# The first microseconds of a two-layer kernel: order of the first requests, layer 0 by chunks of the input, and finer waits

## The reference

```python
x = x + (jnp.einsum('bsd,bdh->bsh', x, W[cat_ids]) + b[cat_ids][:, None, :])      # layer 0

def _dense(x, wi_, wo_):
    return jax.nn.relu(x @ wi_) @ wo_
s0 = _dense(x, swi[0], swo[0])
s1 = _dense(x, swi[1], swo[1])
h = jax.nn.relu(jnp.einsum('bsd,bdf->bsf', x, wi[type_label]))
eo = jnp.einsum('bsf,bfd->bsd', h, wo[type_label])
gate_in = jnp.concatenate([eo[:, 0], s0[:, 0], s1[:, 0]], axis=-1)
w = jax.nn.softmax(jax.nn.relu(gate_in @ g1) @ g2, axis=-1)[:, :, None, None]
x = x + (eo * w[:, 0] + s0 * w[:, 1] + s1 * w[:, 2])                              # layer 1
```

## Time and profile before

| | |
|---|---|
| three runs, median (lowest, highest) | 270.22 us (269.86, 270.35) |
| the profiled execution | 269.85 us, of which the span is 267.9 us |
| TensorE busy | 263.4 us, 98% of the span |
| VectorE, ScalarE, GpSimd busy | 162.3, 149.8, 161.5 us |
| data moved | 18.31 MB, 68 GB/s over the span |
| granted TensorE clock | full in every slice of the span |

### The profile page before, as it was taken

How to read it: one execution, slowest core, us unless ns; L and a number is a source line. 1 busy time by engine, 2 the same in 40 slices (tenths; PEclk the granted TensorE clock), 3 DMA queues, 4 the chain that set the end, 5 groups by cost and what they waited for, 6 DMA issues and landing times.

```text
span 267.9 us, 3482 instructions
## 1 busy us (share of the span) xinstructions
PE 263.4 (98%) x1172; PEld 218.7 (82%) x1172; DVE 162.3 (61%) x246; ACT 149.8 (56%) x265; POOL 161.5 (60%) x170
## 2 busy tenths in 40 slices
PE   8999999999999999999999999999999999999995
PEld 8788888888888888888888888888888888888884
DVE  3879958634654445555345475345476577985664
ACT  2597357665665655765646645546545764645320
POOL 0179989999948949927945626626526528435000
PEclk9999999999999999999999999999999999999999
DMA  5825322022022022012022022022022022000404
GB/s 195 256 100 157 118 78 79 4 78 79 0 81 79 0 78 78 22 60 78 2 78 78 5 76 78 0 79 79 2 78 78 0 81 70 8 0 2 157 1 157
DMA packets 7473, 18.31 MB, mean 68 GB/s; under 512 B 1312, under 2 KB 2080, under 8 KB 7456
## 3 DMA queue, kind: packets, MB, share of 16 engines
q1 hardware_dynamic: 6736, 16.92, 19.2%
q10 hardware_dynamic: 720, 1.18, 1.3%
HBM read 16.00 MB, written 2.10 MB: 68 GB/s over the span
## 4 chain that ended last, share of the span: by engine, by line
PE 96%; DMA 2%; SPq 1%; DVE 0%; issue 0%; ACT 0%; DVEq 0%
PE acc L705 48%; PE chain L705 24%; PE right L705 12%; PE left L705 7%; PE acc L722 4%; DMA w_raw<-cat_w 2%; PE corner L705 1%; SPq L232 1%; DVE x L696 0%; ACT w_hi L363 0%; SPq L234 0%; DVEq L695 0%
## 5 line engine op out<-in xcount | busy, mean ns | idle before, releaser
L275 POOL TENSOR_TENSOR m_lo<-staged,m_hi 128x512 fp32r<-128x512 f32 (+1 forms) x48 | 82.2, 1721 | 78.5 <-ACT m_hi L351 63.9
L705 PE MATMUL acc<-h_hi,m_hi 128*128 128x512 f32 x190 | 73.9, 389 | 0.0
L705 PE MATMUL acc<-h_lo,m_hi 128*128 128x512 f32 x190 | 73.9, 389 | 0.0
L705 PE MATMUL acc<-h_hi,m_lo 128*128 128x512 f32 x190 | 73.9, 389 | 0.0
L375 ACT COPY kept<-chain 128x512 f32<-128x512 f32 x66 | 38.8, 588 | 55.0 <-PE chain L705 55.0
L705 PEld LDWEIGHTS acc<-h_hi,m_hi 128*128 128x128 f32 x190 | 35.7, 188 | 7.4
L705 PEld LDWEIGHTS acc<-h_lo,m_hi 128*128 128x128 f32 x190 | 35.7, 188 | 7.4
L705 PEld LDWEIGHTS acc<-h_hi,m_lo 128*128 128x128 f32 x190 | 35.7, 188 | 7.4
L492 DVE SCALAR_TENSOR_TENSOR h_lo<-left,h_hi 128x512 fp32r<-128x512 f32 x24 | 16.6, 691 | 29.1 <-ACT h_hi L387 29.1
L275 POOL TENSOR_TENSOR staged<-staged 128x128 f32<-128x128 f32 x66 | 31.0, 485 | 1.7
L497 DVE TENSOR_TENSOR left<-left,kept 128x512 f32<-128x512 f32 x22 | 15.3, 695 | 24.3 <-PE left L705 24.3
(11 more groups left out here) (111 smaller groups left out, 442.9 us busy)
## 6 DMA issues: line engine op xcount, KB each, us to landing
staged<-mlp_w SPq DMA_DIRECT2D x22, 512.0 KB, 3.3
x<-x_t ACTq DMA_DIRECT2D x4, 256.0 KB, 4.0
staged<-mlp_w SPq DMA_DIRECT2D x4, 256.0 KB, 3.6
x<-x_t SPq DMA_DIRECT2D x4, 256.0 KB, 5.2
out_t<-x SPq DMA_DIRECT2D x2, 512.0 KB, 3.3
g_sb<-g SPq DMA_DIRECT2D x1, 768.0 KB, 3.8
out_t<-x SPq DMA_DIRECT2D x3, 256.0 KB, 2.3
w_raw<-cat_w SPq DMA_DIRECT2D x4, 128.0 KB, 3.1
```

The lines of the kernel that those rows point to most:

```text
L275: return nc.gpsimd.tensor_tensor(out, a, b, ALU.subtract)
L705: last = nc.tensor.matmul(out[:, columns], half[:, slot, at:at + P], moving[:, columns], start=(start and n == 0), stop=(stop and n == 2), ...
```

## The change

Several edits, all but the last two in the first twelve microseconds:

- **Requests.** ScalarE requests x's second tile only once the first piece of x's first tile has landed, and reads the mlp id itself (a register load), so that it can request wi of group 0, between its two casts of layer 0's weights. SyncE no longer requests that wi.
- **Warm-up.** 12 matmuls instead of 16.
- **Layer 0 by chunks.** For x's first tile (`layer0_first`) both output chunks take input chunk 0 first, in the order hi x hi, hi x lo, lo x hi, each with its own wait, then input chunk 1. For the other three tiles (`layer0`) all products with x_hi come first, those with x_lo last.
- **Finer waits.** x_split becomes a semaphore per chunk. Group 0's wi is cast and split in two halves, row 1 (256 columns, `row1_hi_ready`, `row1_split`) and row 2, and the first direct products wait for part_split 1, 2 and 3 one after another.
- **Who splits.** x_lo of the second tile's second chunk goes from VectorE to GpSimd.
- **Sample 1.** VectorE's first h_lo of group 1 comes ahead of the second x1.
- **Group 3.** Four t_hi casts of the second pair, before split between the ends of groups 2 and 3, all go to group 3, the first two between the casts of hidden sums.

The gate is as it was.

```diff
-WARMUP = 16
+WARMUP = 12
...
-        x_split = [[sem(f"x_split{b}{t}") for t in range(HALVES)] for b in range(B)]
+        x_split = [[[sem(f"x_split{b}{t}{d}") for d in range(DC)] for t in range(HALVES)] for b in range(B)]
...
+        def load_wi(eng, bank, j):
+            eng.dma_start(staged[:, j % 2, A11:RAW_S], group_weights(bank, j, slice(A11, RAW_S))).then_inc(staged_loaded[j % 2], 16)
+
         def load_group(eng, bank, j):
             if j < DIRECT:
 
-                eng.dma_start(staged[:, j % 2, A11:RAW_S], group_weights(bank, j, slice(A11, RAW_S))).then_inc(staged_loaded[j % 2], 16)
+                if j:
+                    load_wi(eng, bank, j)
...
-            split_first(0, False)
+            pool.wait_ge(x_hi_ready[0], 2)
+            subtract(x_part(x_lo, 0, 1, 1), x1_part(0, 1, 1), x_part(x_hi, 0, 1, 1).bitcast(F32)).then_inc(x_split[0][1][1], 1)
+
+            pool.wait_ge(row1_hi_ready, 1)
+            subtract(m_lo[:, 0, A11:A22], staged[:, 0, A11:A22], m_hi[:, 0, A11:A22].bitcast(F32)).then_inc(row1_split, 1)
+            pool.wait_ge(m_hi_ready, first_part(0))
+            subtract(m_lo[:, 0, A22:RAW_S], staged[:, 0, A22:RAW_S], m_hi[:, 0, A22:RAW_S].bitcast(F32)).then_inc(m_split, 1)
             split_first(1, False)
...
-            load_x(act, 0, 0)
+            for d in range(DC):
+                load_x(act, 0, 0, d)
 
             act.wait_ge(ones_ready, 1)
             nc.scalar.activation(table[:], ones[:, 0:1], ACT.Relu)
-            load_x(act, 0, 1)
+            mlp = act.value_load(mlp_ids[0:1, 0:1], min_val=0, max_val=EXPERTS - 1)
+
+            act.wait_ge(x_loaded[0][0][0], 16)
             for d in range(DC):
-                w_hi_of(0, d)
+                load_x(act, 0, 1, d)
+            w_hi_of(0, 0)
+            load_wi(act, bass.ds(mlp, 1), 0)
+            w_hi_of(0, 1)
             for d in range(DC):
                 x_hi_of(0, 1, d)
-            split_first_hi(0, False)
             part_hi_of(0)
+            act.wait_ge(staged_loaded[0], 16)
+            nc.scalar.copy(m_hi[:, 0, A11:A22], staged[:, 0, A11:A22]).then_inc(row1_hi_ready, 1)
             part_hi_of(1)
+            nc.scalar.copy(m_hi[:, 0, A22:RAW_S], staged[:, 0, A22:RAW_S]).then_inc(m_hi_ready, 1)
...
+                if j == 3:
+                    t_hi_of(1, 0)
                 hidden_hi(j, 2)
+                if j == 3:
+                    t_hi_of(1, 1)
...
+                if j == 3:
+                    for n in (2, 3):
+                        t_hi_of(1, n)
-                for pair, first in ((1, 2), (2, 5), (3, 9)):
+                for pair, first in ((2, 5), (3, 9)):
...
-            for d in range(DC):
-                x_lo_of(0, 1, d)
+            x_lo_of(0, 1, 0)
...
             make_x1(1, 0, 0)
-            for i in range(4):
+            hidden_lo(1, 0)
+            make_x1(1, 0, 1)
+            for i in range(1, 4):
                 hidden_lo(1, i)
-            make_x1(1, 0, 1)
...
+            def layer0_first():
+
                 for i in range(DC):
+                    pe.wait_ge(x_first_hi, i + 1)
+                    pe.wait_ge(w_hi_ready, i + 1)
+                    for d in range(DC):
+                        layer0_product(0, 0, i, d, w_hi, x_hi, i == 0, False)
+                    pe.wait_ge(x_split[0][0][i], 1)
+                    for d in range(DC):
+                        layer0_product(0, 0, i, d, w_hi, x_lo, False, False)
+                    pe.wait_ge(w_split[0], i + 1)
+                    for d in range(DC):
+                        last = layer0_product(0, 0, i, d, w_lo, x_hi, False, i == DC - 1)
+                        if i == DC - 1:
+                            last.then_inc(layer0_done, 1)
+
+            def layer0(b, t):
+
+                for i in range(DC):
+                    if t == 0:
+                        pe.wait_ge(w_hi_ready, b * DC + i + 1)
+                        pe.wait_ge(w_split[b], i + 1)
+                    pe.wait_ge(x_hi_ready[b], b * t * DC + i + 1)
+                    for d in range(DC):
+                        layer0_product(b, t, i, d, w_hi, x_hi, i == 0, False)
+                        layer0_product(b, t, i, d, w_lo, x_hi, False, False)
+                for d in range(DC):
+                    for i in range(DC):
+                        if d == 0:
+                            pe.wait_ge(x_split[b][t][i], 1)
+                        last = layer0_product(b, t, i, d, w_hi, x_lo, False, i == DC - 1)
+                    last.then_inc(layer0_done, 1)
...
-                if i == 0:
+                if j == i == 0:
+                    pe.wait_ge(row1_split, 1)
+                    pe.wait_ge(part_split, 1)
+                elif i == 0 or j == 0 and i == 1:
                     pe.wait_ge(m_split, first_part(j))
-                if j == i == 0:
-                    pe.wait_ge(part_split, 2)
                 if j == 0 and i == 2:
                     pe.wait_ge(b12_split, 1)
-                    pe.wait_ge(part_split, 3)
...
                 three(hidden[i], m_hi, blocks[0], slot, *moving[0], True, False)
+                if j == 0 and i in (0, 2):
+                    pe.wait_ge(part_split, i // 2 + 2)
                 three(hidden[i], m_hi, blocks[1], slot, *moving[1], False, True).then_inc(direct_done, 1)
...
-            layer0_of(0)
+            layer0_first()
+            layer0(0, 1)
             for j in range(DIRECT):
                 for i in range(4):
                     direct(j, i)
-            layer0_of(1)
+            for t in range(HALVES):
+                layer0(1, t)
```

More of the change, by code:

```diff
@@ L144, in build @@
         m_hi_ready = sem("m_hi_ready")
+        row1_hi_ready = sem("row1_hi_ready")
+        row1_split = sem("row1_split")
         m_split = sem("m_split")
@@ L251, in _ @@
                         for t in range(HALVES):
-                            load_x(sp, 1, t)
+                            for d in range(DC):
+                                load_x(sp, 1, t, d)
                         load_layer0(1)
@@ L321, in _ @@
                 pool.wait_ge(x_hi_ready[1], d + 1)
-                subtract(x_part(x_lo, 1, 0, d), x1_part(1, 0, d), x_part(x_hi, 1, 0, d).bitcast(F32)).then_inc(x_split[1][0], 1)
+                subtract(x_part(x_lo, 1, 0, d), x1_part(1, 0, d), x_part(x_hi, 1, 0, d).bitcast(F32)).then_inc(x_split[1][0][d], 1)
             split_first(0, True)
@@ L596, in x_lo_of @@
                 dve.wait_ge(x_hi_ready[b], b * t * DC + d + 1)
-                subtract(x_part(x_lo, b, t, d), x1_part(b, t, d), x_part(x_hi, b, t, d).bitcast(F32)).then_inc(x_split[b][t], 1)
+                subtract(x_part(x_lo, b, t, d), x1_part(b, t, d), x_part(x_hi, b, t, d).bitcast(F32)).then_inc(x_split[b][t][d], 1)
             nc.vector.memset(ones[:], 1.0).then_inc(ones_ready, 1)
@@ L604, in _ @@
                 dve.wait_ge(x_first_hi, d + 1)
-                subtract(x_part(x_lo, 0, 0, d), x1_part(0, 0, d), x_part(x_hi, 0, 0, d).bitcast(F32)).then_inc(x_split[0][0], 1)
+                subtract(x_part(x_lo, 0, 0, d), x1_part(0, 0, d), x_part(x_hi, 0, 0, d).bitcast(F32)).then_inc(x_split[0][0][d], 1)
             for d in range(DC):
                 w_lo_of(0, d)
-            for d in range(DC):
-                x_lo_of(0, 1, d)
+            x_lo_of(0, 1, 0)
             dve.wait_ge(bias_loaded[0], 16)
@@ L707, in three, with layer0_product @@
                 return last
-            def layer0(b, t, d):
-                for i in range(DC):
-                    at = i * D + d * P
-                    for n, (w, x) in enumerate(((w_hi, x_hi), (w_hi, x_lo), (w_lo, x_hi))):
-                        if t == d == n == 0:
-                            pe.wait_ge(w_hi_ready, b * DC + i + 1)
-                        if d == n == 0:
-                            pe.wait_ge(x_split[b][t], i + 1)
-                        if t == d == 0 and n == 2:
-                            pe.wait_ge(w_split[b], i + 1)
-                        if b and i == n == 0:
-                            pe.wait_ge(x1_ready, t * DC + d + 1)
-                        last = nc.tensor.matmul(acc[t][d][:], w[:, b, at:at + P], x_part(x, b, t, i),
-                                                start=(i == n == 0), stop=(i == DC - 1 and n == 2))
-                last.then_inc(layer0_done, 1)
+            def layer0_product(b, t, i, d, w, x, start, stop):
+                if b and start:
+                    pe.wait_ge(x1_ready, t * DC + d + 1)
+                at = i * D + d * P
+                return nc.tensor.matmul(acc[t][d][:], w[:, b, at:at + P], x_part(x, b, t, i), start=start, stop=stop)
@@ L825, in _ @@
                 nc.tensor.matmul(left[:, 0:P], ones[:], ones[:], start=True, stop=True)
-            def layer0_of(b):
-                for t in range(HALVES):
-                    for d in range(DC):
-                        layer0(b, t, d)
-            layer0_of(0)
+            layer0_first()
+            layer0(0, 1)
             for j in range(DIRECT):
```

4 lines of the change are left out of this document (2 added, 2 removed).

## The result

| | before | after | ratio (95% interval) |
|---|---|---|---|
| median of nine runs, us | 270.35 | 269.35 | 0.9964 (0.9951 to 0.9977) |
| lowest to highest, us | 269.86 to 270.50 | 268.70 to 269.83 | |

The changed kernel is 1.0 us faster; 1.57 us was forecast. The median of 269.35 us lies inside the stated range, but of the nine runs only the fastest (268.70 us) reached the forecast of 268.7 us. The runs spread over 1.1 us, where those of before spread over 0.6 us. The first is among its slowest.

What follows compares the result with a forecast made beforehand. TensorE bounds the kernel, without gaps from 7.38 us except 0.14 us at 47.14 us. 1.58 (start) + 0.14 (group 3) - 0.15 (collisions) = 1.57 us off, forecast 268.7 us; range 268.2 to 269.7 us.

Steps and rivals of the forecast that it cites:

- Point 1: Start: with x's second tile requested later, layer 0's weights land at 5.3 us, not 6.90; first matmul could start at 5.78.
- Rival B: Start: something else holds the weights, still landing about 6.9 us; first matmul stays at 7.38, time 270.2 us; chance 0.07.
- Point 2: Warm-up: four fewer matmuls save 0.92 us, TensorE free at 5.77 us; pace up at about 5.1 us, layer 0 at full speed.
- the sign that the prediction gave: Layer 0: matmuls 0.4 us apart would show the forecast wrong.
- Point 3: ScalarE's queue: register load runs beside the table load, done by 3.3 us, within the wait for 4.0 us; cost nothing.
- Point 4: x's second tile lands in 3.3 and 3.6 us, covered by 0.7 and 0.9 us; at 5.2 us landing, costs 0.7 us.
- Point 5: Group 0's wi on ScalarE's queue lands at 9.1 us, wanted about 9.9 us; cost nothing, 0.8 us late at 5.2 us landing.
- Point 6: First direct product: VectorE and GpSimd collide, taking turns on SBUF; TensorE loses 0 to 0.3 us, 0.15 us taken.
- Point 7: Later edits: moving t_hi casts brings back 0.14 us at the 47.14 us product; second sample's layer 0 and VectorE order win nothing.
- Rival A: Start: ScalarE's register load ends late, first matmul 6.0 to 6.3 us; gain 1.1 us, time 269.2 us; chance 0.12.
- Rival D: First direct product: start is won, but its chain or a late wi gives back 0.5 to 0.9 us: 269.3 us; chance 0.08.
- Rival C: ScalarE's pointer load takes 3.05 us, x's second tile comes late, TensorE waits 1.05 us: 270.7 us, slower; chance 0.07.

Runs made afterwards that it cites:

- e5: Changed kernel with x's second tile requested at 1.70 us as before the change, with no wait: 271.78 us, ratio 1.0049 to the kernel before.
- a0: The changed kernel run once more with no edit, for a second trace: 269.25 us (one execution).
- e2: Changed kernel, but SyncE requests x's second tile right behind the two weight requests, without ScalarE's wait: 268.56 us, ratio 0.9947 to the kernel before.
- the first trace: First profiled execution of the changed kernel, no further edit: 269.79 us.
- e4: Changed kernel with ScalarE's register load kept, its value unused, and wi of group 0 requested by SyncE: 268.81 us, ratio 0.9950 to the kernel before.
- e1: Changed kernel without ScalarE's register load, SyncE requesting wi of group 0 as before the change: 268.45 us, ratio 0.9942 to the kernel before.
- e6: The kernel before with one edit alone, the four t_hi casts of the second pair moved to group 3: 270.00 us, ratio 0.9992.
- e3: Changed kernel, but SyncE requests nothing of layer 1 until x's second tile has landed: 268.93 us, ratio 0.9958 to the kernel before.
- e11: e1 with row 1's low part made by VectorE instead of GpSimd: 268.49 us, ratio 0.9936 to the kernel before.

## Why the prediction was right, and where it was not

- **Point 1, right.** Weights at 5.3 us forecast, cast from 5.29 us in the trace, first matmul 5.84 us. e5 shows the cause. Rival B fell. In the ten other traces with the later request the two weight requests took 2.3 to 3.2 us, the first of them 2.6 to 3.2 us, and layer 0 began between 5.95 and 6.54 us: a spread in the start that I did not carry into the sum.
- **Point 2, right in one trace, failed in the other.** "The pace has gone up at about 5.1 us" was taken from one execution. In a0 and e2 it had not at 6.1 us; in a0 this cost some 0.65 us. I had named this and given it no price; a0's first two products, 0.5 us apart, are the sign that the prediction gave for it.
- **Point 3, half right.** The load ran beside the table load, but its pointer took 1.7 us, not 0.9 us (SyncE's in the same trace 0.85 us); 4.3 us against the 4.0 us of the wait. Costed at nothing. In the first trace it held the late tile's requests by some 0.3 us; in e4's trace it held nothing, and the 0.28 us of gain between e4 and e1 may be the load or the spread of the weights.
- **Point 4, the step that was mis-sized.** Landing in 3.3 and 3.6 us was taken; 4.6 and 4.9 us, 4.2 and 4.5 us were seen, and 3.4 to 4.1 us without wi behind it. "Only the small weights are ahead of it" looked at what was ahead; what came behind on both queues counted too, as far as the two traces tell. The price at 5.2 us was put at 0.7 us, worked out for the second piece alone; the first, wanted 0.9 us earlier, is what TensorE waited for, 1.01 us at 4.65 us.
- **Point 5, wrong in its second half.** Wi at no cost: with it on ScalarE's queue the gain was 0.37 us less, through the tile ahead of it. It was in time only because the tile was late: it landed at 10.3 us in the first trace, where the forecast wanted it at 9.9 us. That edit is worth undoing.
- **Point 6, right in kind.** The turns cost 0.11 us where the tile is in time (e1: due 11.51 us, begun 11.62 us), 0.15 us was taken. Not seen: x_lo of the second tile stands ahead of x1 on VectorE, which made 0.51 us of it in the first trace and 0.26 us in a0 (x_lo from 9.11 us, x1 from 9.72 us).
- **Point 7, right:** 0.14 us forecast, 0.82 to 0.68 us in the trace, in e6 as well.

The gap between 1.57 and 1.0 us is thus mainly points 2 and 4, with what point 6 adds to them, in shares that change from run to run. The mechanism forecast for the start is shown, and e1 reaches the forecast; that the changed kernel stayed inside the range is owed to the room left for A and D, and not to their reasons. Rival D named the size, and a part of the place (0.51 us at the first direct product), not the tile. Rival A's size, 269.2 us, comes as near, and its sign, requests after 4.3 us, was just met (4.33 us), but ScalarE was free at 5.15 us, before the weights' cast at 5.29 us, so that its reason for a late start fell. Rival C did not come: the pointer load took 1.5 to 1.8 us, not 2.5 us. e5 came out slower than before by another way, a late wi.

## What to carry to other kernels

A request that starts earlier is also a request in front of others: price a moved transfer by what it delays, not only by when its own data comes. A request that waits in a queue behind the arrival of something else inherits its delay: this is wanted for x's second tile, which has time, and it made e5 slow, where wi waited behind the late weights. And where a plan relies on times of a few microseconds at the start (landings, the warm-up's pace), take their spread from several traces; one trace made each cover look 0.7 us thick.

## What the hardware did that I had not expected

- Requests on the two queues land nearly in the order in which they are issued. Wi in e5, alone in ScalarE's queue, took 6.5 us (landed 13.8 us); the request of the same size that SyncE issued 0.14 us before it took 5.7 us (12.8 us), and SyncE's next, at 7.49 us, 6.7 us (14.2 us). The Trainium skill ("DMA: Bandwidth & Descriptors", section "Queues, rings and completion order") has an engine alternate between the queues; by it ScalarE's lone request should have come well ahead of SyncE's queue. No run here shows that.
- After a wait TensorE's first step to the next matmul is 0.33 us (13.03 to 13.36 us), the following 0.24 and 0.23 us, against 0.227 us: there the wait cost 0.12 us more than its own length. In a0, e1 and e3 the first step was 0.34 us too; in e11, which did not wait there, 0.23 us.
- ScalarE's pointer load took 1.5 to 1.8 us in the traces that have it on its queue at 1.7 us, SyncE's took 0.84 to 0.86 us at 0.73 us.
